# Silu, softplus and u in quarters through a PSUM bank in the Mamba stage of a three-stage kernel

## What is computed

```python
def _mamba_block(x, in_w, cw, cb, xw, dw, db, alog, dvec, ow, g, b):
    xm, z = jnp.split(x @ in_w, 2, axis=-1)
    conv = jax.lax.conv_general_dilated(xm.transpose(0, 2, 1), cw, ...)   # causal, 4 taps
    xc = jax.nn.silu(conv.transpose(0, 2, 1) + cb)
    Bp, Cp = jnp.split(xc @ xw, 2, axis=-1)
    dt = jax.nn.softplus(xc @ dw + db)
    A = -jnp.exp(alog)
    def step(h, inp):
        xt, dtt, Bt, Ct = inp
        h = jnp.exp(dtt[..., None] * A) * h + (dtt * xt)[..., None] * Bt[:, None, :]
        y = jnp.einsum('bdn,bn->bd', h, Ct) + dvec * xt
        return (h, y)
    ...
    y = ys.transpose(1, 0, 2) * jax.nn.silu(z)
    return _layer_norm(y @ ow + x, g, b)
```

## Time and profile before

| | |
|---|---|
| median of 3 runs | 6605.51 us (6603.3 to 6608.14) |
| the profiled execution | 6608.62 us, its span 6606.6 us |
| PE, DVE busy | 3922.7 us (59%), 5696.4 us (86%) |
| ACT, POOL busy | 3224.4 us (49%), 4768.9 us (72%) |
| DMA | 694.53 MB, mean 105 GB/s |

### The profile page before, as it was taken

One profiled execution on the slowest core, in us unless ns is written; L12 is line 12 of the kernel. 1 busy time (PEld: TensorE's weight loads), 2 busy tenths in 40 slices (PEclk: granted clock), 3 DMA queues, 4 the chain that ended last, 5 costly groups with the idle time before them and its releaser, 6 DMA issues. The chain is left out here.

```text
span 6606.6 us, 61824 instructions
## 1 busy us (share of the span) xinstructions
PE 3922.7 (59%) x13720; PEld 2255.7 (34%) x13720; DVE 5696.4 (86%) x7287; ACT 3224.4 (49%) x5503; POOL 4768.9 (72%) x3338
## 2 busy tenths in 40 slices
PE   3213213114666767767767667677677676667777
PEld 3102212112333333333334334333333333245556
DVE  3667557654999999999999999999999999967778
ACT  1112102112656666666666666666665665544445
POOL 3352331530999999999999999999999999923334
PEclk9956557555899999999999999999999999988888
DMA  1000000002444444444444444444444444400000
GB/s 26 0 0 10 1 0 1 10 0 60 150 164 161 164 168 159 165 165 161 171 161 166 166 159 166 167 160 167 165 161 167 161 161 170 156 4 2 2 2 2
DMA packets 171432, 694.53 MB, mean 105 GB/s; under 512 B 27969, under 2 KB 34626, under 8 KB 171138
## 3 DMA queue, kind: packets, MB, share of 16 engines
q1 hardware_dynamic: 169608, 688.25, 28.9%
q0 software_dynamic: 1536, 3.14, 0.2%
HBM read 684.77 MB, written 6.55 MB: 105 GB/s over the span
## 5 line engine op out<-in xcount | busy, mean ns | idle before, releaser
L768 POOL TENSOR_TENSOR m_hs<-m_u,m_BC 128x1280 f32<-128x1280 f32 x1024 | 2994.5, 2924 | 69.9 <-DVE m_u L1125 69.9
L984 PE MATMUL m_PS<-m_pr,ident 128*128 128x512 f32 (+1 forms) x6144 | 2500.7, 545 | 900.9 <-DVE m_pr L1108 900.8
L1100 DVE TENSOR_TENSOR_SCAN m_hs<-m_PS,m_hs 128x640 f32<-128x640 f32 x2048 | 2937.7, 1469 | 5.1 <-POOL m_hs L768 3.0
L825 ACT ACTIVATE m_PS<-m_dt,m_A 128x640 f32<-128x640 f32 x2048 | 1613.4, 794 | 911.6 <-DVE m_hs L1100 897.9
L984 PEld LDWEIGHTS m_PS<-m_pr,ident 128*128 128x128 f32 x6144 | 1137.2, 195 | 2164.3 <-DVE m_pr L1108 1126.4
L775 POOL TENSOR_TENSOR m_pr<-m_hs,m_BC 128x384 f32<-128x384 f32 x1024 | 1088.3, 1063 | 183.2 <-DVE m_hs L1100 178.2
L246 POOL TENSOR_TENSOR g_prod<-g_hbuf,g_E 128x128 f32 (+1 forms) x888 | 476.8, 573 | 926.3 <-issue 916.4
L1108 DVE TENSOR_TENSOR m_pr<-m_hs,m_PS 128x896 f32<-128x896 f32 x1024 | 1082.3, 1057 | 7.7 <-DVE m_hs L1100 7.6
L814 ACT COPY m_PS<-m_BC 128x448 f32<-128x448 f32 x1024 | 546.4, 534 | 155.6 <-DVE m_pr L1108 107.1
L291 ACT ACTIVATE g_rstd<-g_rstd 128x100 f32<-128x100 f32 x6 | 1.7, 286 | 925.9 <-DVE g_rstd L538 925.9
L323 PE MATMUL g_TB<-ident,g_nrm 128*128 128x128 f32 x200 | 64.4, 323 | 638.0 <-DVE g_nrm L459 633.3
(11 more groups left out here) (240 smaller groups left out, 4512.7 us busy)
## 6 DMA issues: line engine op xcount, KB each, us to landing
m_BC<-m_scr SPq DMA_DIRECT2D x1024, 640.0 KB, 3.7
m_scr<-m_CB SPq DMA_DIRECT2D x32, 160.0 KB, 4.2
m_hs<-in_cwr SPq DMA_DIRECT2D x4, 512.0 KB, 3.8
out<-f_res SPq DMA_DIRECT2D x20, 64.0 KB, 1.5
m_inw<-in_in_w SPq DMA_DIRECT2D x4, 256.0 KB, 3.8
m_dtw<-in_dw SPq DMA_DIRECT2D x4, 256.0 KB, 3.5
m_xw<-in_xw SPq DMA_DIRECT2D x8, 64.0 KB, 3.6
m_outw<-in_ow SPq DMA_DIRECT2D x4, 128.0 KB, 3.3
```

The costliest lines, as they stand in the source:

```text
L768: pool.tensor_tensor(hs[:, g % RH], u[:, p % 2], BC[:, g % UB:g % UB + 1, 0:S].to_broadcast([P, DT, S]), ALU.mult).then_inc(w_ready, 1)
L825: act.activation(half[d], dt_[:, p % 2, d], ACT.Exp, scale=A[:, l, d, n:n + 1]).then_inc(da_ready, 1)
L984: ins = pe.matmul(Y[:, a:e], ident[:], pr[:, g % RP, a:e], start=False, stop=False, skip_group_check=True)
L1100: v.tensor_tensor_scan(hs[:, g % RH, d, :], half[d], hs[:, g % RH, d, :], 0.0, ALU.mult, ALU.add).then_inc(scan_done, 1)
```

## The change

The two tanhs, the Ln and a new copy of dt are cut in quarters of 320 elements (QW), and ACT writes each into bank `C` instead of `soft`; DVE reads the quarter from there and works on a quarter of `sz`, `xc`, `dt` or `u`. Each quarter is a "take" of bank C: ACT waits until the multiply of the unit has read the bank (`clear`), and `copy_c` of the next unit waits for DVE's quarter. The steps now stand at: z quarters at n = 21 to 24 (with the table load ahead of the first), x quarters at 25 to 28, B and C rows at 29 to 31, zdt at 32 to 37, table load and Abs at 38, Exp at 39, softplus quarters at 40 to 43, u quarters at 44 to 47; the store of B and C moves from 40 to 45. The layer norm's steps move to 48 (STATS), 49, 50, 51 and 52 to 56, scale and shift of the last layer to 58 and 59. The core of the diff:

```diff
-    OUT, TR, ZP, CV, BCP, DTP = 1, 6, 9, 13, 25, 28
-    TANHZ, GATEZ, TANHX, GATEX, STORE = 21, 22, 23, 24, 40
-    STATS, RSTD, ABS, EXPA, LNA, DTS, UMUL = 24, 34, 35, 36, 37, 38, 39
-    STEP, SCALE_R, NORM, SCALE, SHIFT = 40, 41, 42, 48, 49
+    OUT, TR, ZP, CV, GZ, GX, BCP, DTP, SP, UP = 1, 6, 9, 13, 21, 25, 29, 32, 40, 44
+    N_TR, N_ZP, N_CV, N_BCP, N_DTP, NQ = 3, 4, 8, 3, 6, 4
+    ABS, EXPA, STORE = 38, 39, 45
+    STATS, RSTD, STEP, SCALE_R, NORM, SCALE, SHIFT = 48, 49, 50, 51, 52, 58, 59
+    QW = W // NQ
...
+                    if GZ <= n < GZ + NQ:
+                        k = n - GZ
+                        if k == 0:
+                            act.preload_act_table_set("exp_and_others")
+                        act.wait_ge(z_taken, (q + 1) * N_ZP)
+                        act.wait_ge(*clear)
+                        act.activation(C[:, 0:QW], sz[:, q % 2, k * QW:(k + 1) * QW], ACT.Tanh).then_inc(tanhz_ready, 1)
+                        return sz_ready, q * NQ + k + 1
...
+                    if SP <= n < SP + NQ:
+                        k = n - SP
+                        act.wait_ge(expabs_ready, q + 1)
+                        act.wait_ge(*clear)
+                        act.activation(C[:, 0:QW], soft[:, k * QW:(k + 1) * QW], ACT.Ln, bias=1.0).then_inc(ln_ready, 1)
+                        return dt_ready, q * NQ + k + 1
+                    if UP <= n < UP + NQ:
+                        k = n - UP
+                        act.wait_ge(dt_ready, (q + 1) * NQ)
+                        act.wait_ge(*clear)
+                        act.copy(C[:, 0:QW], dt_[:, q % 2].rearrange("p d t -> p (d t)")[:, k * QW:(k + 1) * QW]
+                                 ).then_inc(dt_copied, 1)
+                        return u_ready, q * NQ + k + 1
...
+                    if n == ABS:
+                        act.preload_act_table_set("natural_log_exp_and_others")
+                        act.wait_ge(dtp_taken, (q + 1) * N_DTP)
...
-                    taken = pre_take(p + 1, n) if p + 1 < NLB else None
+                    taken = pre_take(p + 1, n, (prod_ready, g + 1)) if p + 1 < NLB else None
...
-                    if n == GATEZ:
-                        v.wait_ge(tanhz_ready, q + 1)
-                        v.scalar_tensor_tensor(sz[:, q % 2, :], soft[:], 1.0, sz[:, q % 2, :], ALU.add, ALU.mult
+                    if GZ <= n < GZ + NQ:
+                        k = n - GZ
+                        r = slice(k * QW, (k + 1) * QW)
+                        v.wait_ge(tanhz_ready, q * NQ + k + 1)
+                        v.scalar_tensor_tensor(sz[:, q % 2, r], C[:, 0:QW], 1.0, sz[:, q % 2, r], ALU.add, ALU.mult
                                                ).then_inc(sz_ready, 1)
...
+                    if SP <= n < SP + NQ:
+                        k = n - SP
+                        r = slice(k * QW, (k + 1) * QW)
+                        v.wait_ge(ln_ready, q * NQ + k + 1)
+                        v.scalar_tensor_tensor(dtq[:, r], zdt[:, r], 0.0, C[:, 0:QW], ALU.max, ALU.add).then_inc(dt_ready, 1)
+                    if UP <= n < UP + NQ:
+                        k = n - UP
+                        r = slice(k * QW, (k + 1) * QW)
+                        v.wait_ge(dt_copied, q * NQ + k + 1)
+                        v.tensor_tensor(uq[:, r], C[:, 0:QW], xc[:, r], ALU.mult).then_inc(u_ready, 1)
```

More of the change, by code:

```diff
@@ L679, in mamba_stage @@
         bc_stored = sem("bc_stored")
-        tanhz_ready, tanhx_ready = sem("tanhz_ready"), sem("tanhx_ready")
-        abs_ready, expabs_ready, soft_ready = sem("abs_ready"), sem("expabs_ready"), sem("soft_ready")
+        tanhz_ready, tanhx_ready, ln_ready, dt_copied = sem("tanhz_ready"), sem("tanhx_ready"), sem("ln_ready"), sem("dt_copied")
+        abs_ready, expabs_ready = sem("abs_ready"), sem("expabs_ready")
         dt_ready, u_ready = sem("dt_ready"), sem("u_ready")
@@ L762, in w_unit @@
                     if n == 0:
-                        pool.wait_ge(u_ready, p + 1)
+                        pool.wait_ge(u_ready, (p + 1) * NQ)
                     pool.wait_ge(bc_loaded[g % UB], (g // UB + 1) * 16)
@@ L821, in one @@
                         if n == 0 and d == 0:
-                            act.wait_ge(dt_ready, p + 1)
+                            act.wait_ge(dt_ready, (p + 1) * NQ)
                         if g >= 1:
@@ L827, in decay, with pre_take @@
                     return one
-                def pre_take(q, n):
+                def pre_take(q, n, clear=None):
                     l, b = place(q)
@@ L875, in pre_take @@
                         return dtp_taken, q * N_DTP + k + 1
+                    if GZ <= n < GZ + NQ:
[6 more added lines that the diff above has]
+                        return sz_ready, q * NQ + k + 1
+                    if GX <= n < GX + NQ:
+                        k = n - GX
+                        act.wait_ge(cv_taken, (q + 1) * N_CV)
+                        act.wait_ge(*clear)
+                        act.activation(C[:, 0:QW], xc[:, k * QW:(k + 1) * QW], ACT.Tanh).then_inc(tanhx_ready, 1)
+                        return xc_ready, q * NQ + k + 1
+                    if SP <= n < SP + NQ:
[7 more added lines that the diff above has]
+                        act.wait_ge(dt_ready, (q + 1) * NQ)
+                        act.wait_ge(*clear)
+                        act.copy(C[:, 0:QW], dt_[:, q % 2].rearrange("p d t -> p (d t)")[:, k * QW:(k + 1) * QW]
+                                 ).then_inc(dt_copied, 1)
+                        return u_ready, q * NQ + k + 1
                     return None
@@ L879, in pre_more @@
                     l, b = place(q)
-                    if n == TANHZ:
-                        act.preload_act_table_set("exp_and_others")
-                        act.wait_ge(z_taken, (q + 1) * N_ZP)
+                    if n == ABS:
+                        act.preload_act_table_set("natural_log_exp_and_others")
+                        act.wait_ge(dtp_taken, (q + 1) * N_DTP)
                         if q >= 1:
[L884 to L894, removed]
+                            act.wait_ge(ln_ready, q * NQ)
                         act.activation(soft[:], zdt[:], ACT.Abs).then_inc(abs_ready, 1)
@@ L898, in pre_more @@
                         act.activation(soft[:], soft[:], ACT.Exp, scale=-1.0).then_inc(expabs_ready, 1)
-                    if n == LNA:
-                        act.wait_ge(expabs_ready, q + 1)
-                        act.activation(soft[:], soft[:], ACT.Ln, bias=1.0).then_inc(soft_ready, 1)
                 def post_take(q, n):
@@ L951, in post_more @@
                                        scale=rstd[:, j:j + 1], bias=nmr[:, j:j + 1]).then_inc(x_ready, 1)
+                taken = None
                 for n in range(NST):
-                    pre_take(0, n)
+                    taken = pre_take(0, n, taken) or taken
                     pre_more(0, n)
                 act.wait_ge(a_ready, 1)
-                copy_c(0, (dtp_taken, N_DTP))
+                copy_c(0, taken)
                 for g in range(2):
@@ L1028, in pre_piece @@
                         a, e = THIRDS[k]
-                        pe.wait_ge(xc_ready, q + 1)
+                        pe.wait_ge(xc_ready, (q + 1) * NQ)
                         for d in range(DT):
@@ L1119, in pre_step @@
[L1119 to L1126, removed]
+                    dtq = dt_[:, q % 2].rearrange("p d t -> p (d t)")
@@ new lines, in pre_step @@
+                    uq = u[:, q % 2].rearrange("p d t -> p (d t)")
+                    if GZ <= n < GZ + NQ:
[3 more added lines that the diff above has]
+                        v.scalar_tensor_tensor(sz[:, q % 2, r], C[:, 0:QW], 1.0, sz[:, q % 2, r], ALU.add, ALU.mult
+                                               ).then_inc(sz_ready, 1)
+                    if GX <= n < GX + NQ:
+                        k = n - GX
+                        r = slice(k * QW, (k + 1) * QW)
+                        v.wait_ge(tanhx_ready, q * NQ + k + 1)
+                        v.scalar_tensor_tensor(xc[:, r], C[:, 0:QW], 1.0, xc[:, r], ALU.add, ALU.mult).then_inc(xc_ready, 1)
@@ L1132, in post_step @@
                         v.wait_ge(sum_done, (q + 1) * NST)
+                        v.wait_ge(sz_ready, (q + 1) * NQ)
                         v.tensor_tensor(yz[:], Y, sz[:, q % 2, :], ALU.mult).then_inc(yz_ready, 1)
```

7 lines of the change are left out of this document (2 added, 5 removed).

## The result

The changed kernel takes 6496.4 us (median of 4 runs, 6489.8 to 6499.1) against 6605.1 us of the kernel before (4 runs): the ratio is 0.983, 95% interval 0.982 to 0.985, 109 us less. 6498 us was forecast. The profiled execution has a span of 6497.4 us.

A forecast was written before the change was run, and what follows sets the result against it. DVE was taken to set the pace of the Mamba loop, POOL nearly full beside it; -230 removed + 96 quarters + 21 ACT + 6 start = -107 us gave 6498 us, range 6474 to 6540.

The forecast's parts named there:

- Removed, 230 us: DVE in the loop: the four whole-width operation groups, 234.2 us less 4.2 us of overlap, go away.
- Quarters at 0.40 us, 96 us: DVE in the loop: 240 quarters with one PSUM input add 0.40 us each, 96 us, ends 84 and 118.
- ACT hidden behind a quarter: ACT's quarter is ready 0.7 us before DVE asks; copy of C and second decay behind it stay hidden too.
- Table load, 0.7 us: Ahead of the first z quarter: DVE waits 0.7 us for ACT, 15 times, 10.5 us.
- Abs, 0.5 us: Whole-width Abs after the other table load: next decay and DVE 0.5 us later, 15 times, 7.5 us.
- Statistics, 4 us: Layer norm's statistics moved from beside the x gate to unit 48: about 0.25 us each, 4 us in all.
- The start, +6 us: Pass 0's preparation, nothing beside it: ACT-DVE round trips of 1.0 us, 16 us against 9.9.
- Last layer's scaling: Scaling of 640 elements, all-SBUF: up to 10 us in the range if it meets a busy POOL differently.
- Rival 1: Quarters still wait for POOL at z and softplus because of their form: 142 us back, 6640 us; 6%.
- Rival 2: ACT-DVE round trip shows in every quarter, 1.0 instead of 0.40 us, 240 times: +144 us, 6642; 3%.
- Rival 3: POOL takes over the pace, 48 of 64 units at 3.81 us: +38 us, 6536; 9%.
- Rival 4: Uncovered table loads cost a drain more, 15 x 2 x 1.38 = 41 us: 6539; 5%.

The follow-up runs named there:

- the early loads: Changed kernel with both table loads put ahead of ACT's waits for PE's last convolution piece (unit 20) and last zdt piece (unit 37): 6446.1 us.
- the quarters through SBUF: Changed kernel with tanh and Ln quarters written to SBUF tile soft instead of bank C, u quarters still on PSUM: 6535.3 us.
- the silu part alone: Changed kernel with z and x still in quarters through bank C, but softplus (unit 41) and u (unit 42) at full width in SBUF: 6469.3 us.
- the kernel before with its load moved: Kernel before with ACT's second table load moved from unit 34 to 35, ahead of Abs, and RSTD from 34 to 36: 6554.3 us, ratio 0.996.
- At unit 60: Changed kernel with u made at once at unit 60, full width, both inputs in SBUF, instead of four quarters at 44 to 47: 6488.7 us.

## Why the prediction was right, and where not

- *Who sets the pace.* Right. The loop got shorter by 108.8 us by the multiplies' starts, the span by 109.2, and POOL lost its 5.2 us idles (three of 4.5 us remain, at the last layer's scaling).
- *Removed, 230 us.* 98.0 + 23.1 + 88.5 + 21.0 = 230.7 by the units.
- *Quarters at 0.40 us, 96 us.* A quarter lasts 458 to 470 ns (0.45 was worked out) and costs 4.16 - 3.76 = 0.40 us, 240 times.
- *ACT hidden behind a quarter.* Right: x, softplus and u quarters have no idle ahead of them in the loop.
- *Table load, 0.7 us.* 0.66 us, 9.8 us in all. *Abs, 0.5 us.* 0.54 us. *Statistics, 4 us.* 2.6 us. The ends of 0 and 45 us were wide; the gaps of the two table loads are removable, as the early loads showed.
- *The start, +6 us.* From the first tanh to the end of u's preparation both parts together grew by 6.7 us. It cannot be seen in the first scan, which starts 0.72 us later (1662.13 before, 1662.85 after), because the first tanh starts 6.0 us earlier (1624.60 before, 1618.59 after). Between 1606 and 1616 us the convolution pieces ahead of it had a granted clock of 1.00 in the changed kernel (2.4 GHz) and of 0.50 before (1.2 GHz), and followed each other at 1.84 instead of 2.99 us.
- *Last layer's scaling.* Only allowed for in the range, up to 10 us; it cost 7.9 us more (16.7 against 8.7). Two of three calls went from 1.15 to 4.93 us. POOL's tail came 0.41 and 0.43 us behind DVE's start there, 0.37 and 0.39 us before the change; but in the early-loads run it came 0.40 and 0.41 us behind and both calls were short, so what decides between the two stays open.
- *The 2 us between forecast and result.* In part luck. In the loop -230 + 96 + 21 = -113 us was forecast and -108.8 came, mostly for the scaling. Outside it +6 us was forecast and -0.4 came, since the first tanh happened to start 6.0 us earlier in that execution. The two misses nearly cancel.
- *Rival 1 (the form needs POOL to stop)* fell: no quarter waits. By the Trainium skill, SBUF — State Buffer, Who interferes with whom, a DVE instruction with two SBUF inputs contends with a GpSimd instruction that reads SBUF. The trace agrees: in the quarters through SBUF the first z quarter, of the same form and width, lasts 4.13 instead of 0.49 us. *Rival 2* fell with the margin of 0.7 us. *Rival 3* fell too: the unit stays at 3.76 us, and POOL's lag stays below 1.1 us in the median pass, and reaches 2.4 us in the last and 3.7 us in pass 0, where the kernel before had it too. *Rival 4*: the tanh starts 0.01 us behind the table load (2248.30 + 1.28 = 2249.58, 2249.59), so no drain shows. The Trainium skill, ScalarE: Activation LUTs, What ACT_TABLE_LOAD costs, has a drain of about 1380 ns on top of the load; the measurement decides against it here, as the forecast had it.

One reason in it was wrong though the sum was not. The prediction put both waits down to operands in SBUF and their removal to PSUM. That holds for z. For softplus, the quarters through SBUF, the silu part alone and the kernel before with its load moved show that the wait had already gone with the new schedule, by Abs's gap, and that PSUM was not needed; it would have been enough alone, as the early loads show. The 0.5 us gap that the prediction booked as a cost had a use that the prediction did not see.

## What to carry to other kernels

Where a DVE instruction lasts several times its usual length beside a busy GpSimd, look at where GpSimd stands when it starts: give it one input in PSUM, or put it where GpSimd is waiting for DVE, behind a pause or another extra step of DVE. Look too at which instruction GpSimd would be free to start next: it is the rest of its queue that DVE may have to wait for. Before cutting a wide step into pieces, try it whole at such a place, but with a margin: at the edge, single passes fall back to the long wait. When extra steps go, look up what had been hidden beside them: here two table loads, worth 18 us once they stood in ACT's idle time ahead of a wait for TensorE.

## What the runs showed of the hardware

- A DVE instruction with two SBUF inputs beside a busy POOL ended its wait at one of two points in every such case of the ten traces. The first is the end of the product that POOL was running when DVE started: a wait of at most 0.35 us. The second is where POOL had nothing more that it was free to start: 3.7 us and more, with the tail and the next product in between. At unit 60 u waited 1.4 us in 12 cases, because there the tail was all that POOL could start.
- Which of the two it is goes with how far POOL's tail starts behind DVE: at 0.15 to 0.25 us always the first, or no wait at all; at 0.26 to 0.41 us both occur, sometimes in one execution; from 0.43 us on always the second. Where the tail had started before DVE or just then (-0.12 to 0.03 us, four first z quarters through SBUF, held up by the table load), it was the second as well. The order in which the two engines are served was not settled: form and width differ between these cases, and no run changed them one at a time.
- POOL pays when it comes second: where DVE is first, POOL's tail of 1.00 us lasts 2.15 us beside a product of 1.47 us.
- An idle of 0.5 us on the engine that sets the pace took 4.3 us out of an instruction two to three units later, in 12 of 15 passes.
